# Packed pairs of destinations in a count table, and lane one-hots split between VectorE and GpSimd

## The reference

```
pooled = segment_sum(h[col], row, num_segments=N)        # network 0, two layers, batch norms
agg    = segment_sum(h[src], dst, num_segments=N) / deg  # network 1, four layers
aggregated = segment_sum(messages, receivers, ...)       # network 2, messages from h and edge features
agg    = segment_sum(ew[:, None] * h[s], d, ...)         # network 3 ("conv"), two layers
x = x + network_i(relu(layernorm(x)))                    # i = 0..3
```

## Time and profile before

| What | us |
|---|---|
| Median of 3 runs (lowest, highest) | 3236.5 (3234.55, 3239.82) |
| The profiled execution: span from the first to the last instruction (its own device time is not listed apart) | 3240.8 |
| TensorE busy | 2943.5 (91%) |
| VectorE busy | 1047.2 (32%) |
| ScalarE busy | 729.8 (23%) |
| GpSimd busy | 1114.7 (34%) |

### The profile page before, as it was taken

One profiled execution on the slowest core, in us unless ns is written; L12 is line 12 of the kernel. 1 busy time (PEld: TensorE's weight loads), 2 busy tenths in 40 slices (PEclk: granted clock), 3 DMA queues, 4 the chain that ended last, 5 costly groups with the idle time before them and its releaser, 6 DMA issues. The chain is left out here.

```text
span 3240.8 us, 44117 instructions
## 1 busy us (share of the span) xinstructions
PE 2943.5 (91%) x18657; PEld 1740.9 (54%) x18657; DVE 1047.2 (32%) x1860; ACT 729.8 (23%) x1173; POOL 1114.7 (34%) x1012
## 2 busy tenths in 40 slices
PE   1799969997899869999999999999899877999998
PEld 1688835553444335555555555554355664555554
DVE  5899922223200261211111111113311483222122
ACT  4799912223100230000000000001100383011000
POOL 5000013330000004562562663664167101553564
PEclk6899979998999979999999999999899987999999
DMA  7133599994466226666665665664566213665665
GB/s 260 50 129 129 163 244 173 164 170 89 120 147 146 44 66 206 178 171 169 177 175 165 182 178 163 173 173 121 146 181 179 78 54 101 176 180 161 171 170 156
DMA packets 768367, 492.61 MB, mean 152 GB/s; under 512 B 362500, under 2 KB 749836, under 8 KB 767568
## 3 DMA queue, kind: packets, MB, share of 16 engines
q1 hardware_dynamic: 705362, 395.76, 50.5%
q0 software_dynamic: 30112, 62.69, 6.6%
q10 hardware_dynamic: 32702, 31.44, 3.1%
HBM read 334.89 MB, written 76.82 MB: 127 GB/s over the span
## 5 line engine op out<-in xcount | busy, mean ns | idle before, releaser
L2159 PE MATMUL acc<-tbuf,hs 128*128 128x448 fp8e4 x8232 | 1602.0, 354 | 20.0 <-PEq L1242 8.8
L2136 POOL DMA_INDIRECT grow<-hrows,glist x882 | 940.6, 1066 | 791.9 <-PE acc L2183 388.3
L2159 PEld LDWEIGHTS acc<-tbuf,hs 128*128 128x128 f16 x8232 | 801.2, 98 | 762.9 <-issue 52.5
L2298 DVE TENSOR_TENSOR edge_loc<-iota,gdl 128x768 f16<-128x768 bf16 x147 | 140.6, 971 | 743.9 <-PE acc L2183 714.4
L731 PE MATMUL quad<-K,S 128*128 128x196 bf16 x1568 | 278.0, 250 | 17.6 <-DVE K L655 17.6
L1627 PE MATMUL acc<-tbuf,hs 128*128 128x512 fp8e4 (+1 forms) x1300 | 279.6, 369 | 14.9 <-DMA tbuf<-table 14.9
L711 ACT ACTIVATE stage<-quad 128x784 fp8e4<-128x784 f32 x392 | 287.4, 838 | 11.6 <-PE quad L731 5.8
L735 PE MATMUL deg<-K,S 128*128 128x196 bf16 x1568 | 276.8, 248 | 0.0
L1500 PE MATMUL acc<-tbuf,hs 128*128 128x512 fp8e4 (+1 forms) x1300 | 267.4, 369 | 0.7 <-issue 0.7
L2267 ACT ACTIVATE H<-B,vectors 128x448 f32<-128x448 f32 (+2 forms) x56 | 37.4, 668 | 820.3 <-DVE B L2338 820.3
L1500 PEld LDWEIGHTS acc<-tbuf,hs 128*128 128x128 f16 x1300 | 123.6, 98 | 144.4 <-issue 4.3
(11 more groups left out here) (301 smaller groups left out, 2008.5 us busy)
## 6 DMA issues: line engine op xcount, KB each, us to landing
tbuf<-table SPq DMA_DIRECT2D x294, 448.0 KB, 3.6
tbuf<-table SPq DMA_DIRECT2D x294, 336.0 KB, 3.2
table<-stage SPq DMA_DIRECT2D x6, 5488.0 KB, 19.4
grow<-hrows,glist POOLq DMA_INDIRECT x882
hrows<-hs SPq DMA_DIRECT2D x28, 448.0 KB, 4.4
feat<-in_edge_attr_dram ACTq DMA_DIRECT2D x27, 448.0 KB, 6.6
C<-factors ACTq DMA_DIRECT2D x2, 3136.0 KB, 12.5
table<-stage SPq DMA_DIRECT2D x2, 2744.0 KB, 12.2
```

The costliest lines, as they stand in the source:

```text
L2136: g.indirect_dma_start(out=grow[:, n % 2, t, :], out_offset=None, in_=k.hrows[l % 2], in_offset=bass.IndirectOffsetOnAxis(k.glist[:, i // ...
L2159: mm = T.matmul(acc(s, h), rows[l % 2][:, g * US + r, part, :], counts[:, (r - lo) * STRIP + h * HALF:(r - lo) * STRIP + (h + 1) * HALF], ...
L2298: V.tensor_tensor(hot[:, n % 2, :, :], k.iota[:, 0:P].unsqueeze(1).to_broadcast([P, GH, P]), k.gdl[:, i // GU, i % GU * GH:(i % GU + 1) * ...
```

## The change

A window's four destinations are now packed in pairs: an edge to an odd destination counts 256, one to an even destination 1, and both fall into the same column. The key becomes source block x 2 + pair, so NKEY falls from 196 to 98 columns. The weight (1 or 256, the new list `win_odd`) goes into S. The sum, up to 15 + 256 x 15, is written by ScalarE as a 16-bit integer whose two bytes are the two counts; read as fp8, a byte n up to 15 is n x 2^-9 (CODE), so those places that scale sums back use a third column, `k.scales[:, 2]`, larger by 2^9. The quads become octets: eight windows per PSUM buffer, 196 evictions.

S is no longer one tensor_tensor. Each window gets a tensor_scalar of 128 columns with two per-partition scalars (`is_equal` with low, then `mult` with the weight): the first NBP = 5 windows of a batch on GpSimd, the other 9 on VectorE. TensorE waits at each batch for both (`hots`, `lanes`). The checks at the end unpack the two bytes. In the conv chain each layer needs its own matrix twice, scaled with CODE for the table's sums and plain for the gathered ones; TensorE waits for all four copies before its first matmul.

```diff
 WD = 4
-NKEY = NS * WD
+WU = WD // 2
+NKEY = NS * WU
+ODD = 256.0
+CODE = 2.0 ** -9
...
-NQUAD = NBATCH * NBW // 4
+NWE = 8
+NOCT = NBATCH * NBW // NWE
+NBP = 5
...
# first_stage, windows(n), VectorE
-                    V.tensor_scalar(high[at], both[:, :, :, 0], 7, None, ALU.logical_shift_right)
+                    V.tensor_scalar(high[at], both[:, :, :, 0], 6, 0xFFFE, ALU.logical_shift_right, ALU.bitwise_and)
+                    V.tensor_scalar(junk[at].bitcast(I32), both[:, :, :, 1], 1, None, ALU.bitwise_and)
...
-                    V.scalar_tensor_tensor(loc[:, 1, g0:g1, :], high[at], float(WD), dl[at], ALU.mult, ALU.add
+                    V.scalar_tensor_tensor(loc[:, 1, g0:g1, :], dl[at], 1.5, high[at], ALU.is_ge, ALU.add
                                            ).then_inc(loc_ok.h, 1)
+                    V.tensor_scalar(loc[:, 2, g0:g1, :], junk[at].bitcast(I32), ODD - 1.0, 1.0, ALU.mult, ALU.add
+                                    ).then_inc(loc_ok.h, 1)
...
# ScalarE: key and odd lists of a half, then, after the verdict, the low lists (single values)
-                for m in (0, 2):
+                for m in (0, 1):
                     to, at = lists(m)
-                    A.activation(to, at, ACT.Copy)
+                    A.activation(to, at, ACT.Copy).then_inc(loc_out.h, 1)
+                for m in (3, 4):
+                    to, at = lists(m)
+                    A.activation(to, at, ACT.Copy)
                 act.wait_ge(judged.h, judged.at(1))
-                for m in (1, 3):
+                for m in (2, 5):
...
# build_tables, GpSimd
+                for u in range(NHALF * NBATCH):
+                    if u >= 2:
+                        pool.wait_ge(batch_used.h, batch_used.at(u - 1))
+                    for i in range(NBP):
+                        w = u * NBW + i
+                        ins = nc.gpsimd.tensor_scalar(S[:, u % 2, i, :], k.iota[:, 0:SRC_W], k.win_low[:, w:w + 1],
+                                                      k.win_odd[:, w:w + 1], ALU.is_equal, ALU.mult)
+                    ins.then_inc(lanes.h, 1)
# build_tables, VectorE
-                        hot(S[:, q, :, :], k.iota[:, 0:SRC_W], k.win_low[:, at, :], NBW, SRC_W)
+                        for i in range(NBP, NBW):
+                            w = u * NBW + i
+                            V.tensor_scalar(S[:, q, i, :], k.iota[:, 0:SRC_W], k.win_low[:, w:w + 1],
+                                            k.win_odd[:, w:w + 1], ALU.is_equal, ALU.mult)
                         hot(K[:, q, :, :], k.iota[:, 0:NKEY], k.win_key[:, at, :], NBW, NKEY).then_inc(hots.h, 1)
...
# after the last batch: deg is copied to integers, split into its two bytes, added and compared
+                V.tensor_copy(packed[:, :], deg[:, 0:2 * NKEY]).then_inc(split_ok.h, 1)
...
# build_tables, ScalarE
-                            stage[:, b, :, to:to + 4 * WD].rearrange("p b (w d) -> p w b d", d=WD),
+                            pairs16[:, b, :, to:to + NWE * WU].rearrange("p b (w d) -> p w b d", d=WU),
...
# build_tables, TensorE
                         pe.wait_ge(hots.h, hots.at(u + 1))
+                        pe.wait_ge(lanes.h, lanes.at(u + 1))
...
# layer_chain, "conv"
-        own = [k.own_scaled] + ([sb("own", [P, D], F32)] if conv else [])
+        own = [[k.W[n] for n in names] for names in (("a0", "a1"), ("b0", "b1"))]
...
+                if conv:
+                    pe.wait_ge(own_ok.h, own_ok.at(2 * L))
...
-                if conv:
-                    V.tensor_scalar(own[1][:, :], layers[1][0], scale(0, 1), None, ALU.mult).then_inc(own_ok.h, 1)
+                for l in range(L if conv else 0):
+                    for i in range(2):
+                        V.tensor_scalar(own[l][i], layers[l][0], scale(0, l), (CODE, 1.0)[i], ALU.mult, ALU.mult
+                                        ).then_inc(own_ok.h, 1)
```

More of the change, by code:

```diff
@@ L10 @@
 I32 = mybir.dt.int32
+U16 = mybir.dt.uint16
 ALU = mybir.AluOpType
@@ L603, in build_tables @@
         many = sb("many", [P, 2 * NKEY], F32)
+        packed = sb("packed", [P, 2 * NKEY], I32)
+        bytes_of = sb("bytes_of", [P, 2, 2 * NKEY], I32)
+        summed = sb("summed_b", [P, 2 * NKEY], F32)
+        verdict = sb("verdict_b", [P, 4], F32)
         ones = sb("ones_b", [P, 1], F32)
@@ L672, in _ @@
+                dve.wait_ge(split_ok.h, split_ok.at(2))
+                V.tensor_tensor(summed[:, :], bytes_of[:, 0, :], bytes_of[:, 1, :], ALU.add).then_inc(split_ok.h, 1)
+                V.tensor_tensor(many[:, :], bytes_of[:, 0, :], bytes_of[:, 1, :], ALU.max).then_inc(split_ok.h, 1)
+                dve.wait_ge(split_ok.h, split_ok.at(4))
+                V.tensor_reduce(degl[:, :], summed[:, :].rearrange("p (h b d) -> p b h d", h=2, d=WU), AXY, ALU.add
                                 ).then_inc(deg_ok.h, 1)
-                V.scalar_tensor_tensor(many[:, :], deg[:, 0:2 * NKEY], COUNT_MAX + 0.5,
+                V.tensor_reduce(verdict[:, 1:2], summed[:, :], AX, ALU.add).then_inc(judge.h, 1)
@@ L679, in _ @@
-                V.tensor_scalar(k.spilled[:, 1:2], pair[1][:, 0:1], 0.0, None, ALU.is_gt).then_inc(judge.h, 1)
                 dve.wait_ge(judge.h, judge.at(3))
+                V.tensor_scalar(verdict[:, 2:3], pair[1][:, 0:1], 0.0, None, ALU.is_gt)
+                V.tensor_scalar(verdict[:, 3:4], pair[1][:, 1:2], E / P, None, ALU.not_equal).then_inc(judge.h, 1)
+                dve.wait_ge(judge.h, judge.at(4))
+                V.tensor_tensor(k.spilled[:, 1:2], verdict[:, 2:3], verdict[:, 3:4], ALU.max).then_inc(judge.h, 1)
@@ L703, in _ @@
                 A = nc.scalar
+                pairs16 = stage[:, :, :, :].rearrange("p s b c -> p (s b c)").bitcast(U16).rearrange(
+                    "p (s b u) -> p s b u", s=2, u=SU)
                 for h in range(NHALF):
@@ L724, in _ @@
                         pe.wait_ge(hots.h, hots.at(u + 1))
+                        pe.wait_ge(lanes.h, lanes.at(u + 1))
                         for i in range(NBW):
                             w = u * NBW + i
[L727 to L733, removed]
+                            o = w // NWE
+                            if w % NWE == 0 and o >= 3:
+                                pe.wait_ge(moved.h, moved.at(o - 2))
+                            at = w % NWE // (NWE // 2) * 512 + w % (NWE // 2) * NKEY
+                            mm = T.matmul(pair[o % 3][:, at:at + NKEY], S[:, q, i, :], K[:, q, i, :],
+                                          start=(w % (NWE // 2) == 0), stop=True, skip_group_check=True)
+                            if w % NWE == NWE - 1:
                                 mm.then_inc(filled.h, 1)
@@ L739, in _ @@
                 pe.wait_ge(deg_ok.h, deg_ok.at(1))
-                pe.wait_ge(moved.h, moved.at(NHALF * NQUAD))
+                pe.wait_ge(moved.h, moved.at(NHALF * NOCT))
                 T.transpose(pair[0][0:NS, 0:P], degl[:, :], k.idf[:, :]).then_inc(deg_T.h, 1)
-                pe.wait_ge(judge.h, judge.at(1))
-                T.matmul(pair[1][:, 0:1], k.avg[:, :], k.spilled[:, 1:2], start=True, stop=True).then_inc(judge.h, 1)
+                pe.wait_ge(judge.h, judge.at(2))
+                T.matmul(pair[1][:, 0:2], k.avg[:, :], verdict[:, 0:2], start=True, stop=True).then_inc(judge.h, 1)
                 for m in range(4):
@@ L860, in _ @@
                 V.memset(k.scales[:, 1, 0:1], 2.0 ** -LN_SCALE)
+                V.memset(k.scales[:, 2, 0:1], 2.0 ** -LN_SCALE / CODE)
                 V.memset(step[:, 0:1], LN_TOP)
@@ L1381, in _ @@
             V = nc.vector
-            scale = k.scales[:, 1, at_scale:at_scale + 1]
+            scale = k.scales[:, 2, at_scale:at_scale + 1]
             dve.sem_inc(acc_read.h, 2)
@@ L2155, in dense_piece @@
                             if conv:
-                                T.matmul(acc(s, h), own[l][:, :], v[:, chunk_of(s, h)], start=True, stop=False)
+                                T.matmul(acc(s, h), own[l][0], v[:, chunk_of(s, h)], start=True, stop=False)
                         for r in range(lo, hi):
@@ L2176, in gathered @@
                         if conv:
-                            T.matmul(to, own[l][:, :], v[:, (GB0 + b) * P:(GB0 + b + 1) * P], start=True, stop=False,
+                            T.matmul(to, own[l][1], v[:, (GB0 + b) * P:(GB0 + b + 1) * P], start=True, stop=False,
                                      skip_group_check=True)
@@ L2789, in program @@
         with ExitStack() as lists:
-            k.win_low, k.win_key = (lists.enter_context(nc.sbuf_tensor(f"win_{n}", [P, NWIN, 2], BF16))
-                                    for n in ("low", "key"))
+            k.win_low, k.win_odd = (lists.enter_context(nc.sbuf_tensor(f"win_{n}", [P, NWIN], BF16))
+                                    for n in ("low", "odd"))
+            k.win_key = lists.enter_context(nc.sbuf_tensor("win_key", [P, NWIN, 2], BF16))
             first_stage(k, w["x"], w["src"], w["dst"], small_loads(k, w))
```

69 lines of the change are left out of this document (38 added, 31 removed).

## The result

The changed kernel takes 3469.2 us (median of 4 runs) against 3235.7 before: ratio 1.0721, 95% interval 1.0705 to 1.0736, +233.5 us. The forecast was slower, 3291 us, with a range to 3345: the sign was right, the size was not.

The account below looks back on a forecast made before the run. The prediction took ScalarE as the bound before and VectorE after, at 3.10 us a batch. Terms of 51.4 - 0.5 + 0.6 + 3.4 = +54.9 us on 3236.5 gave 3291.4 us, with a range from 3205 up to 3345.

Parts of the forecast that it names:

- What bounds the kernel now: Table stage before the change: ScalarE's evictions, 2.63 us, fill the 2.637 us batch period; VectorE has 0.13 us in hand.
- S on VectorE: Table stage: nine narrow tensor_scalars at a step of 0.224 us make 2.02 us, with K 2.81 us a batch.
- rival A: Table stage: second pointer and port cost nothing, step 0.11 us or so, period 2.2 us, total 3191 us; chance 20%.
- GpSimd's five: GpSimd's one-hots in the table stage: 0.29 to 0.44 us each, 1.5 to 2.2 us for five, under VectorE's 2.8.
- VectorE over 95% busy: Sign that the forecast is right: VectorE this busy from 104 to about 453 us, the table stage.
- The port: Table stage: GpSimd's instructions hold VectorE 0 to 0.8 us per batch, taken as 0.29, for a period of 3.10 us.
- its upper end: Table stage: batch period of 4.26 us, with five whole GpSimd instructions of 0.29 us in VectorE's way.
- The sum: Table stage: 111 batches going from 2.637 to 3.10 us each cost +51.4 us; all terms together +54.9.
- The other terms: Last batch -0.5 us, before the stage +0.6, conv chain's scaled copies +3.4, longer checks after the stage 0.
- C: Rival, much slower: GpSimd's instructions cost 0.44 us or block VectorE whole; period 3.6 to 4.26, 3347 to 3420 us; 12%.
- D: Rival: TensorE's clock falls to 0.50, needing 2.9 us a batch, still under 3.1, so nothing; no chance of its own.
- GpSimd instructions of over 0.5 us: Sign in the table stage that would show the forecast wrong.

Follow-up runs that it names:

- the kernel of the five forms: Changed kernel with VectorE's one-hots only in the first two batches and GpSimd's five instructions each of a different form, against the changed kernel: 3294.0 us, one execution.

## Why the prediction was right or wrong

- **What bounds the kernel now**: the prediction named ScalarE, and the trace before doesn't bear that out. It took the mean step of the evictions, 0.752 us, as ScalarE's own need, and that mean contains its waits: 327 of the 391 steps take 0.70 to 0.72 us, which makes 3.5 x 0.71 = 2.49 us a batch. A wait can hide there, since a record of 845 ns is longer than the step. No batch waited for an eviction: TensorE's first matmul into a quad's buffer starts at least 0.3 us after the eviction that frees it ends, and the only wait for ScalarE's line in its view (the last line below) is that of a matmul behind the last batch. What closes at every batch is a loop of VectorE and TensorE through the two buffers of S and K. In the lines below, from the trace before, TensorE starts a batch 0.06 us after the K that the earlier trace rows has at 201.33 ends, needs 2.54 us for it, and VectorE's S for the batch after the next starts 0.05 us later, at 205.56:

```profile
202.97 0.26 PE L731 MATMUL quad<-K,S 128*128 128x196 bf16 x1
...
205.27 0.24 PE L735 MATMUL deg<-K,S 128*128 128x196 bf16 x1
...
who waited for it (us, times):
  PE quad L741: 1.0, 1
```

  S and K take 2.59 us, so two batches take 2.59 + 0.06 + 2.54 + 0.05 = 5.24 us, or 2.62 each, against a period of 2.637. The error cost the forecast nothing, because VectorE's 2.81 us were above the old period whoever had set it; that was luck. No run relieves ScalarE, VectorE and TensorE one by one. With S kept the packing gave its 87 us, and VectorE is full in that run.
- **S on VectorE**: right. Forecast 0.224 us a step, measured 0.223, a batch of 14 at 3.90 us. That refutes rival A's 0.11 us. The runs show the sum alone, not the 60 ns of a pointer or the 34 of the streaming; the latter was the middle of 0 to 67, so that the last digit fits is partly luck. The 33 ns that the prediction worked out from the Trainium skill (VectorE: DVE Perf Modes, the perf-mode tier table) fit the measured step, but no run here measures the streaming by itself.
- **The step that failed: "GpSimd's five"**, the sentences that one costs 0.29 to 0.44 us by its nearest rows and five stay "under VectorE's 2.8 in either case". An instruction takes 0.79 us with nobody beside it, five 3.88 us. My rows were an affine select without pointers and a tensor_tensor; the tensor_tensor itself was near (398 ns against 440, of which the 0.18 us of start stood in no row). The error was to take other operations of this engine as bounds: the two-pointer, two-operation tensor_scalar has twice the tensor_tensor's time. The upper bound was none. With it the sign "VectorE over 95% busy" failed as well: it was busy 66 to 68%.
- **The port**: right in kind, and for VectorE nearly right in size, but wrong in who pays. I let GpSimd hold VectorE for 0.29 us a batch. In the trace after, nine S take 2.23 us from the first S to K's start, on average over the 112 batches, against 9 x 0.223 = 2.01 alone: 0.22 us. But GpSimd was the later one, so what counts is what VectorE costs GpSimd: 0.76 us a batch, 4.64 less 3.88. The Trainium skill's rule of a lock held for the full instruction (SBUF — State Buffer, Who interferes with whom), which the prediction took word for word for its upper end, does not fit all of this case: had each engine stood still for the whole of the other's instructions, a batch would be 3.88 + 9 x 0.223 + 0.78 = 6.67 us and not 4.64. It fits K beside GpSimd, 0.65 us lost to a streaming of 0.71, and not the nine S, which lose and cost little.
- **The sum**: 111 x 2.00 in place of 111 x 0.463. The other terms were +2.6 for -0.5 (the last batch), 0.4 for 0.6, 3.3 for 3.4 and 0 for 0.
- **The rivals**: C named this way, dear GpSimd instructions, but with 0.44 us for the dear case and 12%; it ended at 3420 us. D: TensorE's clock did fall to 0.50, and at 82 ns a matmul (98 columns at 1.2 GHz) its 28 took 2.3 us, not 2.9 (the price came from 128 columns), hidden behind the other engines wherever the stage ran at 0.50. What would have shown me wrong stood in the list, GpSimd instructions of over 0.5 us and TensorE waiting for the lanes, and both came.

## What to carry to other kernels

An engine's price for an operation is known only from a row of that operation on that engine: where it has none, especially on GpSimd, the nearest rows of other operations are no bound. Here the price was 1.8 times the dearest of them (0.79 us against 0.44). The mean distance of an engine's starts is its own need only where it does not wait, and a wait shorter than the overlap of two records shows in no idle column: follow the starts around the loop of buffers. Count fixed costs per instruction before splitting a wide one: 14 narrow tensor_scalars with two pointers cost 3.1 us for what two wide tensor_tensors do in 1.8. When a change bundles a saving with its price, look for another engine or operand to carry the price: the packing was good, its weight cost least on the smaller operand, in one wide instruction, and partly on the engine that the packing had freed.

## What the runs showed that I had not expected

- GpSimd's tensor_scalar (is_equal, mult, two pointers) costs 364 ns and 3.3 ns a column by its record, against VectorE's 0.223 us in all for 128.
- TensorE's granted clock in this stage differed between the profiled executions, always with 28 matmuls of 98 columns a batch: 1.00 at a batch of 1.80 us, 0.90 at 2.44, mostly 0.82 to 0.84 at 2.58 (0.91 in the stretch shown), 0.74 at 3.08 (the kernel of the five forms), and 0.50 at 3.28, 3.90 and 4.64. The values between are means of stretches at either level. The period does not fix it: of the four executions of the changed kernel one had at least 0.81 in this stage, as worked out above, and the kernels without GpSimd and with three on it had such an execution each (means 0.972 and 0.969 over the whole span, against 0.890 and 0.899 in the profiled ones). What decides it is open. At 0.50 a matmul of 98 columns was spaced 82 ns and the batch still fitted, and the times were the same at either clock, so the low clock cost nothing where another engine was the bound.
- VectorE's records of back-to-back S reach a median of 625 ns in the kernel without GpSimd, while the starts are 0.223 us apart: where queued records overlap, the spacing is the cost and the record is not. The line of that kernel:

```profile
L688 DVE TENSOR_SCALAR S<-iota,win_low,win_odd x1568: 307/625/876, 104.8 to 540.8; 128x128 bf16<-128x128 bf16 x196
```
